# An edge pass whose first layer is one wide product with Wd as weights, a last sum pass that turns sums back ahead of rows, and inverse deviations that are kept

## The reference

```python
def _layernorm(x, axis=-1, eps=1e-05):
    m = jnp.mean(x, axis=axis, keepdims=True)
    v = jnp.var(x, axis=axis, keepdims=True)
    return (x - m) / jnp.sqrt(v + eps)

def _L0_gnn_ref(x, W, b, edge_index):                       # tgt, src = edge_index
    edge_feat = jnp.concatenate([x_i, x_j - x_i], axis=1)   # x_i = x[tgt], x_j = x[src]
    h = jax.nn.relu(edge_feat @ W + b)
    out = jax.ops.segment_max(h, tgt, num_segments=x.shape[0], indices_are_sorted=True)
    return jnp.maximum(out, 0.0)

def _L1_gnn_ref(x, edge_index, W1, b1, W2, b2):             # row, col = edge_index
    norm = deg_inv_sqrt[row] * deg_inv_sqrt[col]
    ...                                                     # coeffs from means of x, a small MLP, a softmax
    result = coeffs[0] * x
    tx = x
    for k in range(1, POLY_DEGREE + 1):                     # POLY_DEGREE = 5
        tx = jax.ops.segment_sum(norm[:, None] * tx[col], row, num_segments=N)
        result = result + coeffs[k] * tx
    return result

x = _layernorm(x + _L0_gnn_ref(x, W, b, edge_index), axis=-1)
x = _layernorm(x + _L1_gnn_ref(x, edge_index, W1, b1, W2, b2), axis=-1)
```

## Time and profile before

| | us |
|---|---|
| runs | 3220.35, 3201.03, 3210.05 |
| median | 3210.05 |
| profiled execution | 3222.55 |
| its span, first to last instruction | 3220.8 |
| TensorE busy | 1841.5 (57%) |
| VectorE busy | 2484.1 (77%) |
| ScalarE busy | 2048.2 (64%) |
| GpSimd busy | 2209.6 (69%) |

### The profile page before, as it was taken

One profiled execution on the slowest core, in us unless ns is written; L12 is line 12 of the kernel. 1 busy time (PEld: TensorE's weight loads), 2 busy tenths in 40 slices (PEclk: granted clock), 3 DMA queues, 4 the chain that ended last, 5 costly groups with the idle time before them and its releaser, 6 DMA issues. The chain is left out here.

```text
span 3220.8 us, 66969 instructions
## 1 busy us (share of the span) xinstructions
PE 1841.5 (57%) x9618; PEld 1106.1 (34%) x9618; DVE 2484.1 (77%) x11593; ACT 2048.2 (64%) x4831; POOL 2209.6 (69%) x2285
## 2 busy tenths in 40 slices
PE   7996666479999996888888883333333332000000
PEld 6884444345555553444444441111111111000000
DVE  8996999999999995888989986455556666555554
ACT  7995877468888883888888873264546401444443
POOL 6777777067777775677777765676666665777776
PEclk9998999889999995778878875555555555555555
DMA  4310444167777774788878875666667633222221
GB/s 143 110 25 20 117 114 114 47 171 212 210 215 214 216 205 100 199 208 202 214 199 216 216 187 125 162 187 181 175 154 207 161 91 79 69 70 68 73 74 53
DMA packets 736782, 467.28 MB, mean 145 GB/s; under 512 B 411287, under 2 KB 622546, under 8 KB 736728
## 3 DMA queue, kind: packets, MB, share of 16 engines
q1 hardware_dynamic: 636084, 321.23, 36.8%
q0 software_dynamic: 75296, 92.22, 12.6%
q10 hardware_dynamic: 25348, 53.33, 5.4%
HBM read 271.38 MB, written 197.86 MB: 146 GB/s over the span
## 5 line engine op out<-in xcount | busy, mean ns | idle before, releaser
L1708 POOL DMA_INDIRECT rows_H<-tab,at_H x424 | 403.9, 952 | 214.6 <-DVE at_H L1761 110.4
L1009 POOL DMA_INDIRECT rec<-edge_x,pos x392 | 394.1, 1005 | 151.0 <-issue 133.0
L1211 POOL DMA_INDIRECT rows_M<-x_ext,at_M x400 | 378.2, 946 | 170.1 <-issue 101.9
L1983 POOL DMA_INDIRECT out_x<-res_L,to_L x384 | 373.7, 973 | 118.7 <-issue 105.1
L1729 ACT ACTIVATE node_H<-node_H,mean,M2n 125x64 f32<-125x64 f32 x800 | 273.6, 426 | 256.6 <-issue 150.5
L1869 PE MATMUL zT_H<-ident,z_H 128*64 128x128 f32 x496 | 150.5, 407 | 444.4 <-issue 351.4
L903 PE MATMUL gps<-table,hiT 125*128 125x400 bf16 x1568 | 307.2, 334 | 1.9 <-ACT table L950 1.1
L380 POOL DMA_INDIRECT edge_x<-in_x,x_at x196 | 204.4, 1043 | 70.2 <-issue 58.8
L563 POOL DMA_INDIRECT edge_x<-in_x,x_at x196 | 189.5, 967 | 67.6 <-issue 59.4
L2000 ACT ACTIVATE std_L<-M_L,coef 128x2 f32<-128x2 f32 x192 | 56.7, 295 | 275.9 <-DVE M_L L2062 275.9
L368 DVE TENSOR_SCALAR ohc<-iota,lo 128x400 bf16<-128x400 f16 x784 | 216.7, 318 | 0.0
(11 more groups left out here) (346 smaller groups left out, 6217.7 us busy)
## 6 DMA issues: line engine op xcount, KB each, us to landing
tab<-given_M SPq DMA_DIRECT2D x98, 384.0 KB
hibc_f<-dst_hi_rows SPq DMA_DIRECT2D x98, 256.0 KB
hibc<-hi_rows SPq DMA_DIRECT2D x98, 256.0 KB
srcbc<-src_rows SPq DMA_DIRECT2D x98, 256.0 KB
tab<-given_M SPq DMA_DIRECT2D x98, 256.0 KB
own<-given_M SPq DMA_DIRECT2D x98, 256.0 KB
own_L<-own SPq DMA_DIRECT2D x192, 128.0 KB
x_ext<-wide SPq DMA_DIRECT2D x100, 241.5 KB
```

The costliest lines, as they stand in the source:

```text
L1009: pool.indirect_dma_start(out=d.rec, out_offset=bass.IndirectOffsetOnAxis(ap=pos[:, s, j:j + 1], axis=0), in_=edge_x[:, i + s * (EB // 2), ...
L1211: pool.indirect_dma_start(out=rows[:, s, j, :], out_offset=None, in_=d.x_ext, in_offset=bass.IndirectOffsetOnAxis(ap=at[:, s, j:j + 1], ax ...
L1708: pool.indirect_dma_start(out=rows[:, s, j, :], out_offset=None, in_=gather, in_offset=bass.IndirectOffsetOnAxis(ap=at[:, s, j:j + 1], axi ...
L1983: pool.indirect_dma_start(out=d.out, out_offset=bass.IndirectOffsetOnAxis(ap=to[:, s, j:j + 1], axis=0), in_=res[:, s, j, :], in_offset=No ...
```

## The change

Four parts.

*Edge pass, first layer.* `Wd` becomes the stationary operand, padded with 64 columns of zeros (`WdP`), and `best` the moving one: one matmul of 512 columns per group (`layer`), which leaves the layer's outcome turned in the lower half of `pT`. VectorE's `first_layer` reads it there and writes `uT`, the lower half of a new tile `both_T`, whose upper half is `sums`; so u and sums are turned back together by four transposes (`both_back`). ScalarE's `give_sums` copies both into `given`, and `make_rows` normalises in place. The order on TensorE, ScalarE and VectorE is changed with it, and some waits name another semaphore.

*Kept inverse deviations.* `rstd` has a place for every group, and the statistics behind the loop read it.

*Placing loop.* On ScalarE `pick` stands ahead of `low`.

*Last sum pass.* In H1 TensorE turns the sums of the round before back ahead of turning this round's rows.

```diff
@@ placing loop, ScalarE
                         high(1 - s, i + s)
                         rows(i + s, 1 - s)
+                        pick(i, s)
                         low(1 - s, i + s)
-                        pick(i, s)
                         factor(i, s)
...
@@ edge pass, TensorE
-            def best_back(i, s):
+            def layer(i, s):
                 settle(pe, k)
                 pe.wait_ge(max_done[s], i + 1)
                 pe.wait_ge(pairT_ready[s], i + 1)
-                two_before(pe, i, s, u_done)
+                pe.wait_ge(sum_done[s], i + 1)
+                pe.matmul(pT[s % 2][:], WdP[:], best[:, s], start=True, stop=True).then_inc(h_done[s], 1)
+
+            def both_back(i, s):
+                settle(pe, k)
+                pe.wait_ge(u_done[s], i + 1)
                 two_before(pe, i, s, far_back)
                 for j in range(GT):
-                    pe.matmul(back[s % 2][:, j, 0:C], best[:, s, j * P:(j + 1) * P], k.Wd[:], start=True, stop=True)
-
-            def sums_back(i, s):
-                settle(pe, k)
-                pe.wait_ge(sum_done[s], i + 1)
-                for j in range(GT):
-                    last = pe.transpose(back[s % 2][:, j, C:2 * C], sums[:, s, j * P:(j + 1) * P], k.ident[0:C, 0:C])
+                    last = pe.transpose(back[s % 2][:, j, :], both_T[:, s, j * P:(j + 1) * P], k.ident[:])
                 last.then_inc(back_done[s], 1)
...
-            pipeline(pe, NG, NS, (4, LAST, product), (8, LAST, sum_rows), (3, LAST, turn), (5, LAST, best_back),
-                     (4, LAST, combine), (5, LAST, sums_back), (4, NG - 1, sum_chunk))
+            pipeline(pe, NG, NS, (6, LAST, both_back), (5, LAST, layer), (4, LAST, product), (8, LAST, sum_rows), (3, LAST, turn),
+                     (4, LAST, combine), (4, NG - 1, sum_chunk))
@@ edge pass, ScalarE
             def give_sums(i, s):
-                act.wait_ge(u_done[s], i + 1)
+                act.wait_ge(back_done[s], i + 1)
                 act.wait_ge(row_away[s], i * 48)
-                act.activation(far_sum[:, s], back[s % 2][:, :, C:2 * C], ACT.Copy).then_inc(far_back[s], 1)
+                act.wait_ge(row_summed[s], i)
+                act.activation(given[:, s, :, C:3 * C], back[s % 2][:], ACT.Copy).then_inc(far_back[s], 1)
...
-                    last = act.activation(row[:, s, j], u[:, s, j], ACT.Identity, scale=rstd[:, b, GT + j:GT + j + 1],
+                    last = act.activation(row[:, s, j], row[:, s, j], ACT.Identity, scale=rstd(n, b, GT + j, 1),
...
-            pipeline(act, NG, NS, (4, LAST, follow), (4, LAST, penalty), (4, LAST, far), (3, LAST, turned),
-                     (7, LAST, make_rows), (4, LAST, pair_turned), (6, LAST, give_sums), (3, NG, deviation))
+            pipeline(act, NG, NS, (6, LAST, give_sums), (4, LAST, follow), (4, LAST, penalty), (4, LAST, far), (3, LAST, turned),
+                     (7, LAST, make_rows), (4, LAST, pair_turned), (3, NG, deviation))
             all_squares(act)
-            act.activation(chunks(k.dev), M2c, ACT.Sqrt, bias=k.eps[0:NP, :], scale=1.0 / C).then_inc(dev_done, 1)
+            act.wait_ge(inverted, 1)
+            act.activation(chunks(k.rn), rstd_c, ACT.Copy).then_inc(dev_done, 1)
@@ edge pass, VectorE
             def first_layer(i, s):
-                dve.wait_ge(back_done[s], i + 1)
-                dve.wait_ge(row_ready[s], i)
-                dve.scalar_tensor_tensor(u[:, s], back[s % 2][:, :, 0:C], 0.0, pair[:, s, :, C:2 * C], ALU.max, ALU.add
+                dve.wait_ge(h_done[s], i + 1)
+                dve.wait_ge(back_done[s], i)
+                dve.scalar_tensor_tensor(uT[:, s], pT[s % 2][C:, :], 0.0, best[C:, s], ALU.max, ALU.add
                                          ).then_inc(u_done[s], 1)
...
-            pipeline(dve, NG, NS, (1, NG - 1, target), (3, NG - 1, mark), (4, NG, inverse), (6, LAST, first_layer), (4, NG, shifts),
-                     (4, LAST, far_factors), (3, NG - 1, far_moments), (6, LAST, row_moments), (3, NG, chunk_moments),
-                     (3, NG, moments), (4, LAST, running_max), (4, LAST, running_sum))
+            pipeline(dve, NG, NS, (1, NG - 1, target), (3, NG - 1, mark), (4, NG, inverse), (4, NG, shifts),
+                     (4, LAST, far_factors), (3, NG - 1, far_moments), (5, LAST, first_layer), (6, LAST, row_moments),
+                     (3, NG, chunk_moments), (3, NG, moments), (4, LAST, running_max), (4, LAST, running_sum))
...
-            link(dve.tensor_scalar(by_group(tu), M2u, 1.0 / C, EPS, ALU.mult, ALU.add))
-            link(dve.reciprocal(ru[:], tu[:]))
-            link(dve.tensor_tensor(by_group(ru), by_group(ru), M2u, ALU.mult))
+            link(dve.tensor_tensor(by_group(ru), M2u, rstd_u, ALU.mult))
+            link(dve.tensor_tensor(by_group(ru), by_group(ru), rstd_u, ALU.mult))
...
-            link(dve.reciprocal(k.rn[:], k.dev[:]))
@@ sum pass, TensorE
-            staggered(pe, rounds_more(pe), NS, (0, turn), (1, turn_back))
+            if final:
+                staggered(pe, rounds_more(pe), NS, (1, turn_back), (0, turn))
+            else:
+                staggered(pe, rounds_more(pe), NS, (0, turn), (1, turn_back))
```

More of the change, by code:

```diff
@@ L181, in build @@
                     k.sums_ps = summed.enter_context(nc.psum_tensor("sums", [KN, BANK], FP32))
-                    k.M2, k.total = (summed.enter_context(nc.sbuf_tensor(nm, [P, NG + 1, NST], FP32)) for nm in ("M2", "total"))
+                    k.M2, k.total, k.rstd = (
+                        summed.enter_context(nc.sbuf_tensor(nm, [P, NG + 1, NST], FP32)) for nm in ("M2", "total", "rstd_all"))
                     k.qs, k.qrow = (summed.enter_context(nc.sbuf_tensor(nm, [P, w], FP32)) for nm, w in (("c_q", 2), ("c_qrow", 1)))
@@ L969, in _ @@
                 rows(LAST, 1)
+                pick(LAST, 0)
                 low(1, LAST)
-                pick(LAST, 0)
                 factor(LAST, 0)
@@ L1092, in edge_pass @@
         st = sb("st", [P, NS, 2 * GT + KN, 6])
[L1093 removed]
+        delta, both, std, shift = (sb(nm, [P, NS, NST]) for nm in ("delta", "both", "std", "shift"))
         far_a, far_b = sb("far_a", [P, NS, GT]), sb("far_b", [P, NS, GT])
@@ L1100, in edge_pass @@
         best = sb("best", [P, NS, GPOS])
-        sums = sb("sums", [C, NS, GPOS])
-        u = sb("u", [P, NS, GT, C])
+        both_T = sb("both_T", [P, NS, GPOS])
+        sums, uT = both_T[0:C], both_T[C:]
+        WdP = sb("WdP", [P, P])
         given = sb("given", [P, NS, GT, 3 * C])
@@ L1109, in edge_pass @@
         back = ps("back", [P, GT, P])
+        h_done = [sem(f"h_done{s}_M") for s in range(NS)]
         ids_in, x_in, chunk_in, ids_ready, gathered = slots("ids_in", "x_in", "chunk_in", "ids_ready", "gathered")
@@ L1125, in edge_pass @@
         M2c, total_c = k.M2[0:NP, 0:NG, 2 * GT:], k.total[0:NP, 0:NG, 2 * GT:]
-        M2u = k.M2[:, 3:3 + LAST + 1, GT:2 * GT]
+        M2u, rstd_u = (kept[:, 3:3 + LAST + 1, GT:2 * GT] for kept in (k.M2, k.rstd))
+        rstd_c = k.rstd[0:NP, 0:NG, 2 * GT:]
         def chunks(kept):
@@ L1180, in load_x @@
                 before, = settle(sp, k, i)
-                sp.wait_ge(u_done[s], before)
+                sp.wait_ge(pT_done[s], before)
                 sp.dma_start(pair[:, s, :, C:2 * C], d.rec[positions(i, s, 1), 0:C].rearrange("(j p) f -> p j f", p=P)
@@ L1455, in inverse @@
                 dve.wait_ge(std_done[s], i + 1)
-                dve.reciprocal(rstd[:, s], std[:, s]).then_inc(small[s], 1)
+                last = dve.reciprocal(rstd(i, s), std[:, s])
+                last.then_inc(small[s], 1)
             def running_sum(i, s):
@@ L1468, in shifts @@
                 dve.wait_ge(small[s], i * SMALL + 5)
-                dve.scalar_tensor_tensor(shift[:, s], group(k.total, i, s), -0.5, rstd[:, s], ALU.mult, ALU.mult
+                dve.scalar_tensor_tensor(shift[:, s], group(k.total, i, s), -0.5, rstd(i, s), ALU.mult, ALU.mult
                                          ).then_inc(shift_done[s], 1)
@@ L1473, in shifts @@
                 dve.wait_ge(chunk_summed[s], i)
[L1474 removed]
+                dve.tensor_tensor(idle_r[:, s], rstd(i, s, 2 * GT, KN)[0:NP], k.idle[:, columns(i, s)], ALU.mult
                                   ).then_inc(idle_ready[s], 1)
[L1477 to L1479 removed]
+            pipeline(dve, NG, NS, (1, NG - 1, target), (3, NG - 1, mark), (4, NG, inverse), (4, NG, shifts),
+                     (4, LAST, far_factors), (3, NG - 1, far_moments), (5, LAST, first_layer), (6, LAST, row_moments),
+                     (3, NG, chunk_moments), (3, NG, moments), (4, LAST, running_max), (4, LAST, running_sum))
             link = Chain(dve, mch)
             all_squares(dve)
+            for s in range(NS):
+                dve.wait_ge(small[s], (NG // NS + (1 if s == 0 else 0)) * SMALL)
+            dve.sem_inc(inverted, 1)
             dve.wait_ge(told, NG)
```

20 lines of the change are left out of this document (11 added, 9 removed).

## The result

| | before | changed |
|---|---|---|
| median of the runs, us | 3214.13 | 3485.31 |
| profiled span, us | 3220.8 | 3486.1 |
| edge pass, first to last running maximum, us | 691.9 | 983.6 |
| last sum pass, first to last `ahead`, us | 295.5 | 264.0 |
| granted clock in the edge pass | 0.81 | 0.67 |

The median before is of four runs, the three above and one more. The kernel is slower: the ratio of the times is 1.0846, with a 95% interval of 1.0807 to 1.0886. The forecast was slower, 3403 in a range of 3250 to 3570.

The account below looks back on a forecast made before the run. Bound in the edge pass: the ScalarE-TensorE loop at 2.4 GHz, TensorE's own work at 1.2. From the profiled 3222.55 us, +227 + 0 + 0 - 34 = 3415.6, or 3403 for a median; range 3250 to 3570.

Parts of the forecast that it names:

- Loop A: Edge pass: today's ScalarE-TensorE loop with `both_back` and `layer` added; 7.50 us at 2.4 GHz, 11.16 at 1.2, deciding there.
- loop B: Edge pass: `layer` waits for ScalarE's copy of the turned x; 8.00 us at 2.4 GHz, deciding there, 9.91 at 1.2.
- +227: Edge pass: us added by the longer loops under a mixed clock, 919 us for 97 periods; mixed-clock case given 0.44.
- a share of 0.45: Edge pass: assumed share at 2.4 GHz, today 0.62; 97 / (0.45/8.00 + 0.55/11.16) = 919 us.
- The row that I leaned on for a lower share: Edge pass before: TensorE stayed at 1.2 GHz through 30 us at 93% busy, taken as evidence for less 2.4 GHz time.
- The clock as what sets the size: Edge pass: TensorE's clock decides the loss, from +84 us at 2.4 GHz throughout to +391 at 1.2 throughout.
- the clock stays up: Rival: TensorE stays at 2.4 GHz in the edge pass, +84 us there, kernel at 3260; chance 0.14.
- VectorE sets the period: Faster rival: VectorE's work closes the edge-pass loop at 6.66 us at the most, kernel at 3130; chance 0.10.
- The wide product: Edge pass, TensorE: one 512-column product (1.05 us at 2.4 GHz) no cheaper than eight narrow ones (1.00); no gain.
- Last sum pass: Wait of `ahead` for the sums goes, GpSimd at 2.50 us a step comes next; -34 us, between -36 and -10.
- Placing loop: `pick` ahead of `low`: 0, between -34 and +15, the latter if TensorE waits 0.15 us longer in each of 98 batches.
- Behind the loop: After the edge loop: two reciprocals and one root saved, hidden by GpSimd's copy; 0, between -5 and 0 us.

Follow-up runs that it names:

- e9: e3 with the copy of the turned x and the deviation both moved ahead of `make_rows` on ScalarE; 3225.42 us, ratio 1.0074.
- e3: The changed kernel with eight products of zeros per period on TensorE, in its pause ahead of `combine`; 3262.37 us, ratio 1.0142.
- e2: The changed kernel with `product` ahead of `layer` and `both_back` on TensorE, and `give_sums` behind `penalty` on ScalarE; 3216.90 us, ratio 1.0005.
- e10: The changed kernel with only `both_back` moved behind `product` on TensorE, and `give_sums` behind `penalty` on ScalarE; 3514.51 us, ratio 1.0978.
- e4: The kernel before with the last pass's new order and six products of zeros per period of the old edge pass; 3159.47 us, ratio 0.9821.
- e1: The kernel before with `pick` ahead of `low`, and sums turned back ahead of rows in the last sum pass; 3184.39 us, ratio 0.9901.
- e7: The kernel before with only `pick` moved ahead of `low` in the placing loop; 3217.71 us, ratio 1.002.
- e5: As e4, with three products of zeros in each period instead of six; 3154.96 us, ratio 0.9844.

## Why the prediction came out as it did

*The loops.* Right at 2.4 GHz, and the part that decided the sign. Loop A was 7.50 by the sum and 7.45 in e9; loop B 8.00 and 7.83 in e3. Taking the steps off the loop, with every instruction kept, gave back 273 of the 292 us of the edge pass (e2). But neither of the two periods forecast for the changed kernel, 8.0 at the one clock and 11.2 at the other, is found in it: from running maximum to running maximum all periods but the first four and the last take 9.9 to 10.4 us, with both clocks in them. Nor does `layer` wait there for the copy of the turned x; loop B comes to light only in e3. The ScalarE wait for `vT`, 2 us and more in each period, did come.

*The size was off by three tenths of the change* (82 of 271 us of the medians): +227 was forecast for the edge pass, +292 it was. The failed step is "I take a share of 0.45, between today's and none", and the formula behind it. The share was 0.34 (clock 0.67), which the formula would have made 97 / (0.34/8.00 + 0.66/11.16) = 954 us, 35 more than the 919 forecast. On the other side loop A at 1.2 GHz was taken too long: `both_back` took 0.91 there for 1.00, `layer` 1.70 for 2.01, and `vT`, where it follows `layer` wholly at 1.2 GHz (e10), 1.91 for 2.08, so that the loop is 2.95 + 0.24 + 1.02 + 1.81 + 0.91 + 1.70 + 1.91 + 0.13 = 10.67 for 11.16, and the formula gives 930. The 54 from there to 984 are the formula's own: it mixes whole periods at either clock. In the trace every period has both, and the time at 2.4 GHz falls where TensorE mostly pauses, while the chain from `pT` to `layer` runs at 1.2. So a third of the time at 2.4 GHz buys only some 0.4 us of the 10.67. The row that I leaned on for a lower share (30 us at 93% busy without a rise) was no guide: the changed kernel's clock rises every 10.25 us out of stretches that are as busy, 6.42 of 6.90 us.

*The clock as what sets the size.* Shown by e3: products of zeros in the pause, the same work otherwise, 225 us less of the edge pass. With the clock up the old edge pass takes 652 us (e4) and the changed one 759 (e3): 107 for the longer loop, and 984 - 759 = 225 for the lost clock, where the old pass lost 692 - 652 = 40 to it (26 if its 678 us in e1 are taken).

*The rival "the clock stays up"* (3260) is e3 almost to the number, 3262, in part by luck: the edge pass was 17 us shorter than the 776 of the sum, and what lies outside it longer. *"VectorE sets the period"* at 6.66 was too low: in e2, with the clock up, VectorE alone is busy 6.9 us in a period (594.38 of 630 us), and with its pauses the round makes 7.33. In the old pass of e4 it was busy 6.3 (547.20 of 580 us in periods of 6.72); the first layer, 0.69 for 0.36, accounts for about half of the difference, the rest is not explained.

*The wide product.* The step that the rows priced at no gain was right: `layer` took 1.10 at 2.4 GHz (e3) where the eight narrow products took 1.00, and 1.70 at 1.2 GHz where they took 1.60. The two are not the same amount of work, though: by their rows the wide one moves 2 x 512 columns and the narrow ones 8 x 64, and half of what the wide one puts out belongs to the zeros of `WdP`. Per column the wide one costs about half, but it has twice the columns, and so nothing was won. The rule of the Trainium skill named there ("Perfetto Trace Analysis", section "Matmuls"), that larger matmuls are more efficient than smaller ones when possible, agrees with the price per column here.

*Last sum pass.* -34 forecast, -31.5 in the trace and -32 to -33 by e1 against e7; GpSimd at 2.50 a step is the bound as predicted.

*Placing loop.* 0 forecast, between -34 and +15; by e7 +6, with an interval of 0 to 13. The 0.15 us a batch behind the +15 is seen in no run. The 8 us by which it ended later in the profile of the changed kernel need not be a price of the swap: from its first to its last, `pick` took 541.5, 543.1 and 549.6 us in the old order (before, e5, e4) and 542.6 to 549.6 in the new one (nine traces, the changed kernel's is 549.6), so the two overlap.

*Behind the loop.* 0 forecast, between -5 and 0, and for the reason given. The last running maximum and the first step of the next stage lie 30.6 us apart in the changed kernel, 34.7 before; without this part (before, e1, e4, e5, e7) it is 32.3 to 37.8 us, with it (the other seven traces) 28.9 to 35.0, in the mean 2.5 less, but the ranges overlap. VectorE's statistics do end sooner, 18.9 to 22.1 us behind the last running maximum for 26.6 to 32.4; yet in all twelve traces the next stage starts 6.6 us behind the end of GpSimd's last copy, so GpSimd sets it and the saving stays hidden.

What stays open: why the clock keeps step with the period as it does. The runs show that it rises and stays when the pause is filled or the chain is cut, and no more.

## What to carry to other kernels

Before a step is moved, write down the loop from one period to the next, with every engine in it, and see whether the step lands between two of its members; a step that was hidden in a pause costs its whole length there. Where a pause of TensorE lies on that loop, ask in the same breath what the granted clock does: here the lost clock cost twice what the longer loop did, and a few products of zeros in it made even the kernel before some 25 us faster, 0.8% (e4 against e1). When one wait is removed and the mean does not move, look for a loop over two periods.

## What the hardware showed that was not expected

The granted clock and the kernel's period fell into step (3.4 us up, 6.8 down, period 10.25), so that a share of time at a clock says little about the share of work done at it. In e2 it stayed at 2.4 GHz with TensorE busy 454.3 of 630 us (72%), while the changed kernel lost it with 696.7 of 887 (79%): busy share over a long stretch did not tell the two apart. And GpSimd, shown with 74% busy in the edge pass before (22.65 of 30.70 us), was close to full there: 0.94 us of work and 0.30 of issue for each gather leave no more than 76% to be shown.
